# A vision layer with a token tower, dense and routed experts on one core: an earlier clear, ReLUs ahead of exponentials, a routing chain moved by one dense block

## What is computed

```python
h = _L0_tok_ref(x, ...)
# attention over all rows
f = _l2norm(feats)
attn = softmax(f @ f.T)
feats = _l2norm(f * 0.8 + (attn @ f) * 0.2)
h = layernorm(h + feats)
# mixture of 8 experts, one per token, with a capacity
idx = argmax(softmax(x @ gate_w + gate_b))
pos = rank of the token in its expert's queue, over all copies
y = relu(x @ w1[idx] + b1[idx]) @ w2[idx] + b2[idx]
y = y * prob * (pos < C)
h = layernorm(h + y)
```

## Time and profile before

| | us |
|---|---|
| median of three runs | 378.65 |
| the three runs | 374.99, 378.75, 378.65 |
| profiled execution | 374.87 |
| its span, first to last instruction | 372.7 |

### The profile page before, as it was taken

How to read it: one execution, slowest core, us unless ns; L and a number is a source line. 1 busy time by engine, 2 the same in 40 slices (tenths; PEclk the granted TensorE clock), 3 DMA queues, 4 the chain that set the end, 5 groups by cost and what they waited for, 6 DMA issues and landing times. The chain is left out here.

```text
span 372.7 us, 6609 instructions
## 1 busy us (share of the span) xinstructions
PE 306.8 (82%) x2238; PEld 181.1 (49%) x2238; DVE 277.7 (75%) x769; ACT 185.6 (50%) x353; POOL 101.9 (27%) x110
## 2 busy tenths in 40 slices
PE   3899536299998999999999998848999879999910
PEld 3669216286553554645546554314546555454500
DVE  2693596779999799998998999824535863895695
ACT  1452024256566656466575564345454662777600
POOL 2420000046254213626236154322422242300000
PEclk9999555589999999999999999969869977999985
DMA  7690000039000000000000001200000000103051
GB/s 191 155 179 2 0 1 2 1 136 404 10 0 3 0 2 3 13 3 10 5 0 14 0 10 27 46 12 5 12 13 3 6 12 7 50 2 76 1 148 37
DMA packets 11266, 14.90 MB, mean 40 GB/s; under 512 B 7014, under 2 KB 8749, under 8 KB 11234
## 3 DMA queue, kind: packets, MB, share of 16 engines
q1 hardware_dynamic: 8898, 10.61, 10.3%
q10 hardware_dynamic: 1152, 2.95, 3.0%
q0 software_dynamic: 1184, 0.94, 1.0%
HBM read 6.05 MB, written 8.54 MB: 39 GB/s over the span
## 5 line engine op out<-in xcount | busy, mean ns | idle before, releaser
L1809 DVE TENSOR_TENSOR esum<-esum,ex 128x896 f32<-128x896 f32 x77 | 86.0, 1117 | 12.0 <-ACT ex L793 7.9
L1125 PE MATMUL pR<-ex,V 128*64 128x448 f32 x336 | 83.4, 556 | 7.6 <-ACT ex L793 7.6
L793 ACT ACTIVATE ex<-pS 128x896 f32<-128x896 f32 (+1 forms) x63 | 55.3, 885 | 27.9 <-PE pS L1108 26.3
L1106 PE MATMUL pS<-QH,KHL 128*64 128x448 f16 x237 | 47.3, 359 | 0.6 <-DVE QL L1609 0.6
L1108 PE MATMUL pS<-QL,KHL 128*64 128x448 f16 x237 | 47.1, 357 | 0.0
L624 POOL TENSOR_TENSOR ps_small<-ps_small,half_neg 112x4 f32<-112x4 f32 x12 | 20.7, 1723 | 64.1 <-DVE ps_small L1678 41.2
L677 POOL DMA_INDIRECT results<-xtile x21 | 21.5, 1026 | 55.2 <-DVE xtile L1863 51.1
L793 ACT ACTIVATE ex<-pR 128x896 f32<-128x896 f32 (+1 forms) x28 | 24.9, 889 | 16.7 <-PE pR L1108 15.8
L1125 PEld LDWEIGHTS pR<-ex,V 128*64 128x64 f32 x336 | 24.7, 138 | 16.7 <-ACT ex L793 8.4
L899 ACT ACTIVATE ex<-pS,eb1s 128x448 f32<-128x448 f32 x32 | 19.5, 639 | 17.3 <-PE pS L1287 15.0
L1106 PEld LDWEIGHTS pS<-QH,KHL 128*64 128x64 f16 x237 | 16.2, 111 | 18.2 <-issue 13.1
(11 more groups left out here) (323 smaller groups left out, 620.6 us busy)
## 6 DMA issues: line engine op xcount, KB each, us to landing
records<-xtile SPq DMA_DIRECT2D x7, 693.0 KB, 8.1
ew<-in_L_ffn_w SPq DMA_DIRECT2D x3, 512.0 KB, 8.6
img<-in_x SPq DMA_DIRECT2D x6, 196.0 KB
img<-in_x ACTq DMA_DIRECT2D x6, 196.0 KB
xtile<-records SPq DMA_DIRECT2D x21, 33.0 KB, 1.8
out_h<-big SPq DMA_DIRECT2D x6, 112.0 KB
out_h<-big ACTq DMA_DIRECT2D x6, 112.0 KB
pk<-in_packed ACTq DMA_DIRECT2D x1, 523.0 KB, 5.6
```

The source lines that it names most:

```text
L793: nc.scalar.activation(o, i, ACT.Exp, scale=1.0 / (SPLIT * SPLIT)).then_inc(s_exp, 1)
L1106: MM(o[r], KHL[:, k0 + r.start:k0 + r.stop], QH[:, j * BLK:(j + 1) * BLK], start=True, stop=False)
L1125: i = MM(pR[t * D:(t + 1) * D, 0, 0:BLK], tile_values(2 * p + t), ex[:, g % NE, t], start=(p == 0), stop=(p == LAST - t))
L1809: i = V_.tensor_tensor(total, total, ex[:, g % NE], ALU.add)
```

## The change

1. GpSimd clears `hot_t` behind `dropped(4)` in its loop over blocks, not behind the whole loop (one block sooner). The wait in front of it asks for the same count of exponentials (13 x 4).
2. In block 6, ScalarE runs `relus(p - 9)` in front of the exponential of pair p, not behind it.
3. The chain of block 6's routing moves. `take_hot(1)` and `turn_choices(1)` go from n = 8 to n = 9, with `take_hot(1)` ahead of `h2_rows(6)`. `post_cols(6)`, `copy_columns(6)`, `post_gate(6)` and `gate_exp(6)` go from the first dense block into the second; `dropped_rows(6)` goes to the third; `turn_columns(2)`, `take_x16(2)`, `turn_choices(2)`, `take_hot(2)` go from experts 2 and 3 to experts 4 to 7 of the second block. `keep_dropped(0, ...)` goes from experts 4, 5, 6 to 2, 3, 6. VectorE runs `post_low(6)` and `post_route(6)` behind the last `take_pair`.
4. `queue_bases` goes from expert 1 of the second block to expert 1 of the third, and `pBase` from `pS` bank 1 to `pR` bank 3.
5. `rows_back(0)` goes from expert 5 of the second block to expert 3, into `pS` bank 1; `rows_back(1)` from expert 5 of the third block to expert 2. Their waits are exchanged to match.
6. VectorE runs `take_rows(0)` and the final norm of range 0 ahead of the rank steps, not behind them.

```diff
--- before.py
+++ after.py
@@ -377,8 +377,8 @@
 
             return (pR[:, 1] if b == 1 else pR[:, 0])[:, 0:BLK]
 
-        pBase = pS[0:ROWS, 1, 0:2 * E]
-        pBack = [pM_[0:ROWS, 0:GW * D].rearrange("p (w d) -> p w d", d=D) for pM_ in (pR[:, 3], pS[:, 1], pR[:, 3])]
+        pBase = pR[0:ROWS, 3, 0:2 * E]
+        pBack = [pM_[0:ROWS, 0:GW * D].rearrange("p (w d) -> p w d", d=D) for pM_ in (pS[:, 1], pS[:, 1], pR[:, 3])]
         pPos = pR[0:ROWS, 3, 480:480 + E]
         pCnt = pR[0:1, 3, 496:496 + E]
         pM = pR[:, 3, :]
@@ -686,8 +686,9 @@
                 if 0 < j < last - 1:
                     scatter_rows(j - 1)
                 dropped(j)
-            pool.wait_ge(s_exp, NPAIR * 4)
-            nc.gpsimd.memset(hot_t, 0.0).then_inc(s_clear, 1)
+                if j == LAST_BLOCK - 2:
+                    pool.wait_ge(s_exp, NPAIR * j)
+                    nc.gpsimd.memset(hot_t, 0.0).then_inc(s_clear, 1)
             for t in range(NTILE):
                 scatter_results(t)
 
@@ -786,6 +787,8 @@
                     if g >= NE:
                         act.wait_ge(s_av, g + 1 - NE)
                         act.wait_ge(s_es, g + 1 - NE)
+                    if j == LAST_BLOCK and p >= FIRST_TURN + 2:
+                        relus(p - FIRST_TURN - 2)
                     if p < LAST:
                         o, i = ex[:, g % NE], scores_at(g)[:, :, 0:BLK]
                     else:
@@ -804,8 +807,6 @@
                     if j and p == (LAST - 1 if j == LAST_BLOCK else LAST):
                         copy_columns(j - 1)
                     if j == LAST_BLOCK and p >= FIRST_TURN:
-                        if p >= FIRST_TURN + 2:
-                            relus(p - FIRST_TURN - 2)
                         take_columns(p - FIRST_TURN)
                         if p == 9:
                             h2_rows(j - 1)
@@ -924,36 +925,37 @@
             gate_exp(last - 1)
             for n in range(TURNED, len(TP)):
                 relus(n)
-                if n == TURNED + 3:
-                    copy_columns(last)
                 keep_expert(n - TURNED + 2)
                 if n + 2 < len(TP):
                     take_columns(n + 2)
                 if n == TURNED + 1:
                     dropped_rows(last - 1)
                     take_x16(1)
-                if n == TURNED + 2:
+                if n == TURNED + 3:
+                    take_hot(1)
                     h2_rows(last)
-                    take_hot(1)
             for i in range(len(TP) - TURNED + 2, E):
                 keep_expert(i)
-            gate_exp(last)
             for e in range(E):
                 keep_expert(E + e)
                 if e == 0:
                     take_dense(0)
                 if e == 1:
-                    dropped_rows(last)
-                if e == 2:
+                    copy_columns(last)
+                if e in (2, 3, 6):
+                    keep_dropped(0, (2, 3, 6).index(e))
+                if e == 4:
+                    gate_exp(last)
+                if e == 5:
                     take_x16(2)
-                if e == 3:
+                if e == 7:
                     take_hot(2)
-                if e in (4, 5, 6):
-                    keep_dropped(0, e - 4)
             for e in range(E):
                 keep_expert(2 * E + e)
                 if e == 0:
                     take_dense(1)
+                if e == 1:
+                    dropped_rows(last)
                 if e in (2, 3, 4):
                     keep_dropped(1, e - 2)
                 if e == 5:
@@ -1236,7 +1238,7 @@
             def queue_bases():
 
                 pe.wait_ge(s_cnt_in, 1)
-                pe.wait_ge(s_yv, NTILE)
+                pe.wait_ge(s_hott, 2 * len(DENSE))
                 MM(pBase[:, 0:E], packed_at("base", ROWS), rk_small[:, 0], start=True, stop=True)
                 MM(pBase[:, E:2 * E], packed_at("image", ROWS), rk_small[:, 0],
                    start=True, stop=True).then_inc(s_cnt, 1)
@@ -1318,11 +1320,11 @@
 
                 pe.wait_ge(s_yacc, b + 1)
                 if b == 0:
-                    pe.wait_ge(s_hott, 2 * len(DENSE))
+                    pe.wait_ge(s_yv, NTILE)
                 elif b == 1:
+                    pe.wait_ge(s_y, 1)
+                else:
                     pe.wait_ge(s_cntc, 1)
-                else:
-                    pe.wait_ge(s_y, 1)
                 for w in range(GW):
                     i = MM(pBack[b][:, w], yacc[:, b % 2, w * ROWS:(w + 1) * ROWS], packed_at("stack"), start=True, stop=True)
                 i.then_inc(s_yb, 1)
@@ -1387,12 +1389,8 @@
                 hidden_pair(n, experts[n])
                 if n == TURNED + 1:
                     turn_columns(1)
-                if n == TURNED + 2:
+                if n == TURNED + 3:
                     turn_choices(1)
-                if n == TURNED + 3:
-                    post_cols(last)
-                if n == TURNED + 4:
-                    post_gate(last)
                 i = n - TURNED + 2
                 if i % 2 == 0 and i > 2:
                     dense_outputs(0, i // 2 - 1)
@@ -1407,21 +1405,25 @@
             dense_outputs(0, E // 2 - 1)
             for e in range(E):
                 dense_expert(E + e)
-                if e == 1:
-                    queue_bases()
+                if e == 0:
+                    post_cols(last)
                 if e == 2:
+                    post_gate(last)
+                if e == 3:
+                    rows_back(0)
+                if e == 4:
                     turn_columns(2)
-                if e == 3:
+                if e == 6:
                     turn_choices(2)
-                if e == 5:
-                    rows_back(0)
                 if e % 2 and e > 1:
                     dense_outputs(1, (e - 3) // 2)
             for e in range(E):
                 dense_expert(2 * E + e)
                 if e == 0:
                     dense_outputs(1, E // 2 - 1)
-                if e == 5:
+                if e == 1:
+                    queue_bases()
+                if e == 2:
                     rows_back(1)
                 if e % 2 and e > 1:
                     dense_outputs(2, (e - 3) // 2)
@@ -1961,23 +1963,21 @@
                 if n == TURNED + 1:
                     post_weight(last - 1)
                     last_dropped()
-                if n == TURNED + 3:
-                    post_low(last)
-                if n == TURNED + 4:
-                    post_route(last)
             take_pair(len(TP) - 1)
+            post_low(last)
+            post_route(last)
             rank_counts()
             post_weight(last)
-            rank_bases()
-            rank_own()
-            rank_image()
-            keep_copies()
+            take_rows(0)
             dve.wait_ge(ld_y[0], 16)
             q = ENDS[0]
             step(V_.tensor_tensor(fin_t[:, q], y_all[:, q], h2_all[:, q], ALU.add))
             final_center(0)
             final_norm(0)
-            take_rows(0)
+            rank_bases()
+            rank_own()
+            rank_image()
+            keep_copies()
             for c in range(COPIES):
                 choose(0, c)
             take_rows(1)
```

## The result

| | before | after |
|---|---|---|
| median | 378.7 us (374.99 to 378.78, 4 runs) | 357.3 us (356.24 to 359.73, 4 runs) |
| ratio | 1 | 0.9468 [0.9403, 0.9532] |
| profiled execution | 374.87 us, span 372.7, granted clock 0.897 | 359.73 us, span 357.6, granted clock 0.903 |

Faster by 5.3%. The forecast was 357.0 us in 349.8 to 364.0. The profiled execution is the slowest of its four, though, and on its own footing the forecast was 355.1, which it misses by 4.6 us. So the steps have to be gone through one by one.

A forecast was written before the change was run, and what follows sets the result against it. Bounds: a late GpSimd clear stopping four engines, TensorE's lower-clock spells and waits, VectorE's tail. 374.87 - 12.3 (block 6) - 7.5 (dense blocks and tail) = 355.1 us; half of 3.8 added for the median gives 357.0, range 349.8 to 364.0.

The forecast's parts named there:

- The clear: Block 6, GpSimd's memset one block sooner: the next scores starts at 241.6 instead of 248.97, 7.4 us gained.
- ReLUs first: Block 6's score periods: ReLUs ahead of the exponential give 4.1, 4.45, 4.3 against 5.41, 5.35, 5.42, 3.3 us gained.
- The last period: Scores 12 to the end of block 6's values: 5.9 us at the upper clock against 8.4; a fall adds 0.85.
- The spell at the end of block 6: Lower clock from 271.7 before: taken to stay because the change keeps that instruction sequence, so 0 gained behind the values.
- The first dense block: TensorE loses its waits, block 6's turn and gate, and the last lower-clock spell: ends 10.0 us earlier.
- the second rival: The lower-clock spell in the first dense block stays: about 5.1 us less gained, 360.2 us; chance 0.19.
- Second block and tail: Moved chain makes VectorE idle 4 + 4 us before post_weight(6); the 7.15 us gap goes; net 7.5 us with the first dense block.
- the unedited stretch: End of block 6's value products to its blending sums: 11.1 us at the lower clock as before, 0 gained.
- the allowance of half of 3.8 us: Whole execution: half of the upper timed runs' 3.8 us excess over the profiled one, added to 355.1 to give 357.0.
- clear gives nothing: take_hot(0) in block 6 waits as long on something else, so 7.4 us comes back: 362.5 us; chance 0.03.
- slower: TensorE stays at the lower clock through the second and third dense blocks: 390.0 us; chance 0.03.
- Full clock throughout: Both lower-clock spells around the end of block 6 go: 352.8 us on the profiled footing; chance 0.19.

The follow-up runs named there:

- the change again: The changed kernel unedited, run a second time on the first chip: 360.28 us, 0.9708 of before.
- the change's third trace: The changed kernel unedited, run a third time, on the third chip: 364.84 us, 0.9648 of before.
- the two with `post_weight` late: The changed kernel with post_weight(6) behind range 0's final norm and queue_bases right behind the second dense block, on two chips: 363.33 us (0.9663) and 361.0 us (0.9556).
- the wide products: The changed kernel with ten pairs of unused score-sized products added around block 6's last outputs and gate: 365.57 us, 0.9694 of before.
- the other two of the second chip: The changed kernel with VectorE's old order put back, 381.72 us; and with the last tile's outputs behind expert 7's chunks, 368.72 us.

## Why the prediction was right

The clear did what the prediction says, the ReLUs and the moved chain did it in kind, and the clock's spells went their own way. Of the signs that the prediction named, the memset, the short idle of `take_hot(0)` and the lost gap of 7 us came; the last value product at 261.2, the periods of at most 4.5 and the upper clock behind 285 did not.

**The clear: right.** TensorE's second `scores` starts at 241.53, forecast 241.6. What the edit is worth over a whole execution is less sure: 10.1 us by medians, 6.1 by the ratio and 5.4 to 6.7 at equal clock when it is added to before; 9.1 and 3.9 when it is taken out of after. The step left one thing out. In both traces with the stall the clock falls inside it, 3.9 and 1.8 us into TensorE's 6.4 us of idleness, which the forecast had only as the length of the work at either level.

**ReLUs first: right in kind, 2.0 us too large.** 1.3 for 3.3. The step took three old periods of 5.41, 5.35, 5.42. The first of them lay partly in the spell of 244.4 to 251.3, and was dear by the clock, not by the order; in the old order at the upper level it takes 4.55. The three come to 15.17, not 16.18: 1.0 of the miss. The walk's new periods were 1.0 short (12.85 against 13.87), nearly all in the first two. In the first, small steps add up: scores 0.88 for 0.8, hidden products 0.63 for 0.5, then 0.32 to the ReLUs (243.04 to 243.36) and 0.14 from their end to the outputs, for which the walk leaves 0.2 together. In the second, the row step of block 5 holds ScalarE to 248.02, 0.45 us beyond the hidden products' end, and the ReLUs begin 0.3 later. The third has 0.14 ahead of the ReLUs and is 4.37 for 4.3.

**The last period: 8.00 for 6.75.** The prediction called the old one "nearly all at the lower" level; by its own row, 3.3 of the 8.4 us ran at 1.00. The eight hidden products alone take 1.0 (259.44 to 260.44), still at the upper clock, where the walk put 0.5; in before they took 0.85 at that clock (270.10 to 270.95), which could have been read. The gate, 1.3 instead of 0.8, was met by the fall. The spell isn't the reason for the first: without one, in the change again, they take the same (262.24 to 263.23), 0.12 us apart where those of the other periods are 0.06 apart. Why, no row tells. The gate and the values without the spell: 263.23 to 265.01, 1.8 us, against 3.0 in after, so the fall cost 1.2 and not 0.85. The whole period without it is 6.82 us there, where the walk had 5.9: 0.9 of the miss is the walk's, 0.35 the fall's.

**The spell at the end of block 6: as taken, for a wrong reason.** The forecast let it stay because the order of instructions stays. In after it stayed. Of eleven other traces with that order of products there, five, the change again among them, do not have it. The Trainium skill, "TensorE: Matmul & The Clock Gate", section "Why this matters for your kernels", ties the fall to idle gaps. By that rule after should not have fallen at 260.9, where no gap since 249.6 is over 0.31 us, nor at 294.9, where the largest is 0.41; these rows speak against it as the only cause. Longer gaps are met both ways: falls came in or behind the stall of 6.43 us and gate waits of 2.38 and 3.05, and none behind the 2.35 us of two traces. What brings a spell without a gap stays open; it is not the program alone.

**The first dense block: the waits went, the spell did not.** 27.5 for 24.4 us, 3.1 of the miss. The step tied the last spell to the 2.35 us gap ahead of it. That tie is wrong both ways: the waits are 0.22, 0.41 and 0.73 now and the spell is there, 6.9 us long, and the clear alone has the gap without the spell. This is the second rival, "the spell in the first dense block stays", and in the profiled execution it took its 5.1 us less what the shorter spell spares. In the change again, without spells, the forecast's own case happened: 24.6 us for 24.4.

**Second block and tail: right.** 11.8 for 11.45 us to `post_weight(6)`, VectorE idle for 7.03 + 3.78 where 4 + 4 were forecast (the 3 us more are TensorE's delay in the first dense block, counted above; in the change again it is 4.15 + 3.78), the 7.15 gap gone, 3.9 us of cover for `rows_back(2)` where 4.5 were given. What the 7.5 us net hid is its mixture: 5.1 of it was the spell. At equal clock two traces give 2.9, against 7.5 - 5.1 = 2.4; beside the late ReLU, on the third chip, the times give nothing.

**The sum.** On the profiled execution: 15.1 us for 19.8. Short by 2.2 in block 6, 3.1 in the first dense block, 0.35 in the second; 0.5 to the good in the unedited stretch and 0.5 from `post_weight(6)` to the end. The median came out at 357.3 because two things stand on the other side: the profiled execution of after was 2.4 us above its median, and the allowance of half of 3.8 us, made because that of before was at the lower end of its runs, added 1.9. Those 3.8 us go with the clock, at least in part. The four executions of after had spans of 357.6, 354.1, 355.8 and 354.6 us at 0.903, 0.922, 0.923 and 0.922; the one at the lower clock is the long one. So the walk was 4.6 us too hopeful and the footing 4.3 us off the other way, and that they cancel to 0.3 is luck.

The rival "clear gives nothing" fell with the row at 238.51; "slower" with granted 1.00 from 301.8 on. "Full clock throughout" happened in another execution, the change again, at 357.75 us where 352.8 were forecast: 2.7 of the 5 us lie ahead of the choices' turn, the rest in block 6's periods and behind.

## What to carry to other kernels

Price a stall and the clock spells behind it apart: take an edit's worth between rows of equal granted clock, and give the spells a price per microsecond from two executions of one kernel (0.35 to 0.4 us of span for 1 us here). Do not take a wait ahead of a spell in one trace as its cause: look for the same wait in a second trace. A wait that is moved back on one engine needs work in front of it on the engine that reads it: the later `queue_bases` without VectorE's new order took back all of the gain. Where engines stand in a ring of narrow hand-overs, the ReLUs began 0.14 to 0.32 us after their products' end, where the walk let them start as the products end. Moving one link (ReLUs ahead of the exponential) gives back only the wait that the others don't hold.

## What the runs showed of the hardware

- The granted clock is not the program's alone. The same instructions in the same order ran once with spells of 6.8 and 6.9 us, once with 3.4 us from 251.0 and 6.9 us from 295.3, and once with none from 240 us to TensorE's end. The clock fell at 260.9 with no gap over 0.31 us in the 11 us ahead, and stayed up behind a gap of 2.35 us in two traces, while before fell behind the same gap.
- One ReLU at the start of the second dense block, always the second one, began 1.4 to 4.4 us after the product that it reads had ended: 1.4 in the change's third trace and with the clear put back, 2.2 and 4.4 in the two with `post_weight` late, 2.8 with the wide products, 2.7 in the other two of the second chip. In after, the change again and its variant with the ReLUs behind the exponential, and in all traces with the old chain, it isn't there. So the edits of the second chip don't bring it; whether the moved chain is needed for it is open, since the old chain ran beside it on one chip only. Waits of TensorE of 1.0 to 3.1 us, mostly for the gate, follow it, and in six of these seven traces a spell. Its cause wasn't found, and no run was made for it.
- Between executions, the choices' turn of block 6 comes anywhere from 237.8 to 242.3 us, ahead of nearly every edit. For the changed kernel alone it was 237.9, 240.7 and 237.8: executions of one kernel differ by 2.9 us before the changed order begins.
